# Angle tables spread by TensorE, and the first query projection from rounded parts, in a Trainium2 transformer layer

## The reference

```python
def layer(x):                                  # x is (2, 1024, 512)
    Q = heads(x @ Wq.T + bq)                   # 32 heads of 16
    K = heads(x @ Wk.T + bk)                   # 8 heads of 16
    V = heads(x @ Wv.T + bv)
    Q, K = (t * cos + rot_half(t) * sin for t in (Q, K))
    w = softmax(Q @ repeat(K, 4).T / 4)
    x = layernorm(x + merge(w @ repeat(V, 4)) @ Wo.T + bo)
    h = silu((x @ gate_w.T) * gate_s) * ((x @ up_w.T) * up_s)
    return layernorm(x + (h @ down_w.T) * down_s)
```

## Time and profile before

| | us |
|---|---|
| median of 3 runs | 1018.65 (1018.28 to 1018.89) |
| the profiled execution | 1020.25, with a span of 1018.3 from its first to its last instruction |
| TensorE busy in the span | 1007.7 (99%) |
| VectorE / ScalarE / GpSimd busy | 797.5 / 665.6 / 274.0 |
| first maxima tile on TensorE | 25.51 after the span's start |

### The profile page before, as it was taken

One profiled execution on the slowest core, in us unless ns is written; L12 is line 12 of the kernel. 1 busy time (PEld: TensorE's weight loads), 2 busy tenths in 40 slices (PEclk: granted clock), 3 DMA queues, 4 the chain that ended last, 5 costly groups with the idle time before them and its releaser, 6 DMA issues.

```text
span 1018.3 us, 15671 instructions
## 1 busy us (share of the span) xinstructions
PE 1007.7 (99%) x5852; PEld 533.1 (52%) x5852; DVE 797.5 (78%) x1132; ACT 665.6 (65%) x1345; POOL 274.0 (27%) x284
## 2 busy tenths in 40 slices
PE   9999999999999999999999999999999999999996
PEld 4643435334444333443444433333358888888885
DVE  6999797999787999779899999999713666462635
ACT  5279796888787989779667788888862430222221
POOL 3461030241255541246310063466000001000002
PEclk9999999999999999999999999999999999999999
DMA  6184417234225521444150447331439112221011
GB/s 229 62 214 123 109 55 203 64 93 91 55 84 123 92 85 39 86 112 100 36 81 12 121 140 186 86 104 59 157 107 228 51 42 59 66 66 17 0 42 44
DMA packets 64290, 94.82 MB, mean 93 GB/s; under 512 B 37520, under 2 KB 37776, under 8 KB 62128
## 3 DMA queue, kind: packets, MB, share of 16 engines
q1 hardware_dynamic: 63920, 93.49, 34.9%
q10 hardware_dynamic: 288, 0.26, 0.1%
HBM read 53.88 MB, written 27.00 MB: 79 GB/s over the span
## 4 chain that ended last, share of the span: by engine, by line
PE 96%; DVE 2%; DMA 0%; issue 0%; POOL 0%; DVEq 0%; POOLq 0%
PE PS L478 30%; PE PV L497 25%; PE PSA L567 16%; PE PS L584 6%; PE PSA L456 6%; PE PS L400 4%; PE PS L523 2%; PE PSA L523 2%; PE PV L584 2%; PE PSA L400 2%; DVE nmx L1007 1%; PE PS L437 1%; DMA A<-in_wqk 0%; PE PV L437 0%; PE PS L567 0%; DVE nmx L1003 0%
## 5 line engine op out<-in xcount | busy, mean ns | idle before, releaser
L798 ACT ACTIVATE Bn<-PS 128x512 f32<-128x512 f32 x1128 | 536.2, 558 | 86.5 <-PE PS L478 73.7
L456 PE MATMUL PSA<-Kt,Qt 48*128 48x512 f32 x1010 | 382.9, 459 | 0.5 <-DVE nmx L1007 0.4
L478 PE MATMUL PS<-Qt,Kt 50*128 50x512 f32 x1128 | 381.9, 434 | 0.0
L478 PEld LDWEIGHTS PS<-Qt,Kt 50*128 50x128 f32 x1128 | 183.3, 184 | 302.7 <-ACT Bn L798 277.1
L1003 DVE TENSOR_REDUCE nmx<-PSA 128x1 f32<-128x512 f32 x488 | 310.7, 678 | 29.8 <-PE PSA L456 29.8
L1007 DVE TENSOR_REDUCE nmx<-PSA 128x1 f32<-128x1024 f32 x261 | 317.4, 1218 | 17.9 <-PE PSA L456 15.0
L497 PE MATMUL PV<-Bn 128*32 128x512 f32 x2048 | 272.8, 605 | 0.0
L456 PEld LDWEIGHTS PSA<-Kt,Qt 48*128 48x128 f32 x1010 | 173.0, 183 | 8.7 <-issue 2.2
L567 PE MATMUL PSA<-x1Th,wr 128*128 128x512 f32 x344 | 135.3, 393 | 0.0
L567 PE MATMUL PSA<-x1Tl,wr 128*128 128x512 f32 x344 | 134.3, 390 | 0.0
L834 ACT ACTIVATE sg<-PSA,gs 128x512 f32<-128x512 f32 x43 | 29.7, 690 | 128.1 <-PE PSA L567 128.1
(11 more groups left out here) (174 smaller groups left out, 899.6 us busy)
## 6 DMA issues: line engine op xcount, KB each, us to landing
Qt<-pscr SPq DMA_DIRECT2D x90, 128.0 KB, 5.2
A<-in_wf SPq DMA_DIRECT2D x11, 768.0 KB, 5.8
wr<-A SPq DMA_DIRECT2D x33, 256.0 KB, 2.9
pscr<-A SPq DMA_DIRECT2D x16, 512.0 KB, 3.5
vscr<-Bn SPq DMA_DIRECT2D x32, 256.0 KB, 2.7
Kt<-pscr SPq DMA_DIRECT2D x90, 64.0 KB, 2.8
A<-A SPq DMA_DIRECT2D x16, 256.0 KB, 3.6
Bn<-vscr SPq DMA_DIRECT2D x8, 512.0 KB
```

The costliest lines, as they stand in the source:

```text
L456: op = e.matmul(slot_pair(s)[:, h, :], Qt[n % 3][p:p + NC_, g % 2, 128 * qt:128 * qt + 128], Kt[n % 3][p:p + NC_, 512 * h:512 * h + 512], ...
L478: e.matmul(score_tile(i)[:, cols], Kt[n % 3][rows, 128 * kt:128 * kt + 128], Qt[n % 3][rows, g % 2, 512 * qh + cols.start:512 * qh + cols. ...
L798: e.activation(Pb[c % NP_][:, cols], score_tile(score_bank[c, p])[:, cols], ACT.Exp, scale=0.25).then_inc(*act_exp.next(piece(c, p)))
```

## The change

- **Angles.** `sinT` and `cosT` (1 MB, four loads) are no longer loaded. A table of 24 rows by 2304 bf16 numbers is (110 KB, two loads on ScalarE's queue): eight frequencies, each value as a sum of three bf16 addends, and a 0, 1, -1 pattern. Four bf16 products on TensorE (`spread_angles`, 128 by 512 each) spread and add them into PSUM, and ScalarE copies each to `sinT` or `cosT` (`keep_angles`).
- **Filling products.** A third one of 192 columns is added to the two of 512.
- **Order.** Both halves of K come first (the angle products among them), then both of Q0. The value products of two tiles come in whole ahead of the picks, not in pieces around them.
- **Q0 from parts.** Q0's eight plain products become split ones, 24 records. They need `xh0`/`xl0` of all eight pieces and the parts of `wq0`, which are now made in the opening: `round_w(0)` by ScalarE, `low_x(0)` and `low_x(1)` by VectorE, the other six `low_x` and `low_w(0)` by GpSimd, in a row.
- **Low part of K, half 0** (`low_first(0, 0)`) moves from VectorE to GpSimd, behind that row; `low_w(1)` follows without its wait for VectorE. Four of VectorE's six memsets of `Kt` move to GpSimd.

```diff
-                if b == 0 and m in (0, 4):
+                if b == 0 and m == 4:
                     w.wait_ge(*landed[f"wq{m}"].at())
                     w.wait_ge(*landed[f"xT{h}{k}"].at())
                     pairs = [(wqk[:, m, k, :], xT[:, h, k, :])]
                 elif b == 0:
-                    w.wait_ge(*pool_split.at(("x0", h, k)))
+                    w.wait_ge(*(dve_split if 4 * h + k < 2 else pool_split).at(("x0", h, k)))
                     w.wait_ge(*pool_split.at(("w0", m)))
                     pairs = [(v[m][:, k, :], t[4 * h + k][:, :]) for v, t in ((wh0, xh0), (wl0, xh0), (wh0, xl0))]
...
+            def spread_angles(h):
+                w.wait_ge(*landed[f"angle{h}"].at())
+                for j in range(2):
+                    c = 256 + 1024 * h + 512 * j
+                    e.matmul(bank(2 * h + j), angle[0:24, 128 * j:128 * j + 128], angle[0:24, c:c + 512],
+                             start=True, stop=True).then_inc(*pe_angle.next((h, j)))
...
-            for _ in range(2):
-                e.matmul(PV[:, :], Vflat[:, 0:128], Vflat[:, 0:512], start=True, stop=True)
-            fill(0, 0, 0, 1, 2, 3)
+            for n in (512, 512, 192):
+                e.matmul(PV[:, 0:n], Vflat[:, 0:128], Vflat[:, 0:n], start=True, stop=True)
+            fill(0, 0, 0, 1)
+            spread_angles(0)
+            fill(0, 0, 2, 3)
+            fill(0, 1, 0)
+            spread_angles(1)
+            fill(0, 1, 1, 2, 3)
             fill(1, 0, 0, 1, 2, 3)
-            fill(0, 1, 0, 1, 2, 3)
-            fill(1, 1, 0)
-            pick(0, 0, 0, PSA[:, 0, :], dve_lo.at((0, 0)))
-            fill(1, 1, 1, 2, 3)
-            value_rows(0, 0, 3, (0, 1))
+            fill(1, 1, 0, 1, 2, 3)
+            bank_free[0:4] = [act_angle.at((h, j)) for h in range(2) for j in range(2)]
+            value_rows(0, 0, 3)
+            pick(0, 0, 0, PSA[:, 0, :], pool_lo.at((0, 0)))
+            value_rows(0, 1, 3)
+            pick(0, 1, 0, PSA[:, 1, :], dve_lo.at((0, 1)))
             for a in range(2):
                 pick(1, 0, 2 + 2 * a, bank(2 * a), dve_lo.at((1, 0)))
-            pick(0, 1, 0, PSA[:, 1, :], dve_lo.at((0, 1)))
...
-            value_rows(0, 0, 3, (2, 3))
-            value_rows(0, 1, 3)
...
+            def keep_angles(h):
+                for j, t in enumerate((sinT, cosT)):
+                    w.wait_ge(*pe_angle.at((h, j)))
+                    e.copy(t[:, 512 * h:512 * h + 512], bank(2 * h + j)).then_inc(*act_angle.next((h, j)))
...
-            round_x(0, 1, 2, 3, 4, 5, 6, 7)
+            round_x(0, 1)
+            keep_angles(0)
+            round_x(2)
+            round_w(0)
+            round_x(3, 4, 5)
+            keep_angles(1)
+            round_x(6, 7)
             round_first(0, 0, dve_rope.at((0, 0)))
...
+            round_w(1)
+            round_first(0, 1, dve_rope.at((0, 1)))
+            evacuate_last()
             round_first(1, 0, dve_rope.at((1, 0)))
...
+            low_x(0, 1)
             turn_pairs(0, 0)
+            turn_pairs(0, 1)
             turn_pairs(1, 0)
-            low_first(0, 0)
-            turn_pairs(0, 1)
+            low_first(0, 1)
             low_first(1, 0)
-            low_first(0, 1)
+            place(Kt[0][64:64 + NC_, 512:1024], PSA[64:64 + NC_, 1, :], pe_pick.at((0, 1, 0)), ("k", 1))
             place(Qt[0][:, 1, 0:512], bank(2), pe_pick.at((1, 0, 4)), ("q", 0, 1))
-            place(Kt[0][64:64 + NC_, 512:1024], PSA[64:64 + NC_, 1, :], pe_pick.at((0, 1, 0)), ("k", 1))
...
-            low_x(0, 1, 2, 3)
-            w.wait_ge(*dve_lo.at((0, 1)))
+            for i in (1, 2):
+                for p in (32, 96):
+                    w.wait_ge(*pool_one.at())
+                    e.memset(Kt[i][p:p + 18, :].bitcast(F32), 1.0).then_inc(*pool_one.next())
+            w.wait_ge(*pool_one.at())
+            low_x(2)
+            low_w(0)
+            low_x(3, 4, 5, 6, 7)
+            w.wait_ge(*act_hi.at(("first", 0, 0)))
+            e.tensor_tensor(lo_r[0][:, 0:512], qraw[0][:, 0:512], hi_r[0][:, 0:512].bitcast(F32), ALU.subtract).then_inc(
+                *pool_lo.next((0, 0)))
             low_w(1)
-            low_x(4, 5)
...
             load_rows(0)
             load(wqk[:, 0], wqk_d[:, 0], "wq0")
-            load_angles(0)
             load_rows(1)
             load(sel_in.rearrange("p (m c) -> p m c", m=6), sel_d, "sel")
-            load_angles(1)
```

More of the change, by code:

```diff
@@ L83, in post_ln_layer @@
         wo = sb("wo", [128, KT, 512])
+        base_x1a = 32 * ((nc.sbuf_base + 31) // 32)
         x1a = sb("x1a", [128, 8, 512])
@@ L137, in post_ln_layer @@
               for m, p in enumerate((84608, in_a(2048), in_a(0), in_a(512), 82560))]
+        angle = at("angle", base_x1a - base, [128, 2304], BF16)
         xh0 = [at(f"xh0{j}", 66176 + 2048 * j, [128, 512], F32R) for j in range(8)]
@@ L141, in post_ln_layer @@
         wh0 = {m: at(f"wh0{m}", 82560 + 4096 * (m - 1), [128, KT, 128], F32R) for m in (1, 2, 3)}
+        wh0[0] = at("wh00", 36864, [128, KT, 128], F32R)
         wl0 = {m: at(f"wl0{m}", 84608 + 4096 * (m - 1), [128, KT, 128], F32R) for m in (1, 2, 3)}
+        wl0[0] = at("wl00", 38912, [128, KT, 128], F32R)
         ath = [at(f"ath{k}", in_a(3072 + 1024 * k), [128, 1024], F32R) for k in range(KT)]
@@ L904, in scalar @@
             load(wqk[:, 4], wqk_d[:, 4], "wq4")
+            load(angle[0:24, 0:1280], angle_d[:, 0:1280].bitcast(BF16), "angle0")
             load(bqk[:, :], bqk_d, "bqk")
-            round_x(0, 1, 2, 3, 4, 5, 6, 7)
+            load(angle[0:24, 1280:2304], angle_d[:, 1280:2304].bitcast(BF16), "angle1")
+            round_x(0, 1)
[5 more added lines that the diff above has]
+            round_x(6, 7)
             round_first(0, 0, dve_rope.at((0, 0)))
@@ L960, in turn_pairs @@
                 w.wait_ge(*landed["bqk"].at())
-                w.wait_ge(*landed[f"sin{h}"].at())
-                w.wait_ge(*landed[f"cos{h}"].at())
+                w.wait_ge(*act_angle.at((h, 0)))
+                w.wait_ge(*act_angle.at((h, 1)))
                 for p in (0, 64):
@@ L970, in turn_pairs, with low_x @@
                 e.tensor_tensor(raw, raw, qrot, ALU.subtract).then_inc(*dve_rope.next((i, h)))
+            def low_x(*js):
+                for j in js:
+                    h, k = divmod(j, KT)
+                    w.wait_ge(*act_split.at(("x0", h, k)))
+                    e.tensor_tensor(xl0[j][:, :], xT[:, h, k, :], xh0[j][:, :].bitcast(F32), ALU.subtract).then_inc(
+                        *dve_split.next(("x0", h, k)))
             def low_first(i, h):
@@ L1337, in rope @@
                 w.wait_ge(*swapped_in[j % 2].at(j))
-                for h in range(2):
-                    w.wait_ge(*landed[f"cos{h}"].at())
-                    w.wait_ge(*landed[f"sin{h}"].at())
+                w.wait_ge(*act_angle.at((1, 1)))
                 e.tensor_tensor(raw, raw, cosT, ALU.mult).then_inc(*pool_rope.next((j, "cos")))
@@ L1453, in gpsimd @@
             e.memset(Vflat[:, 512:2208], 1.0).then_inc(*pool_one.next())
-            low_x(0, 1, 2, 3)
-            w.wait_ge(*dve_lo.at((0, 1)))
+            for i in (1, 2):
+                for p in (32, 96):
+                    w.wait_ge(*pool_one.at())
[7 more added lines that the diff above has]
+                *pool_lo.next((0, 0)))
             low_w(1)
-            low_x(4, 5)
             raw, qrot, cos, sin = cols_of(1, 1)
             w.wait_ge(*act_ev.at("swapped"))
-            w.wait_ge(*landed["sin1"].at())
-            w.wait_ge(*landed["cos1"].at())
+            w.wait_ge(*act_angle.at((1, 1)))
             e.tensor_tensor(raw, raw, cos, ALU.mult).then_inc(*pool_cs.next("cos"))
@@ L1468, in gpsimd @@
                 *pool_cs.next("lo"))
-            low_x(6, 7)
             low_w(2)
@@ L1529, in load_rows @@
                     load(xT[:, h, k, :], xT_d[0, h, :, k, :], f"xT{h}{k}")
-            def load_angles(h):
-                c = slice(512 * h, 512 * h + 512)
-                load(sinT[:, c], sin_d[:, c], f"sin{h}")
-                load(cosT[:, c], cos_d[:, c], f"cos{h}")
             def write_parts(b, m, i, hi, lo):
@@ L1712, in sync @@
             load(ident[:, :], id_d, "id")
+            w.wait_ge(*pool_lo.at((0, 0)))
             w.wait_ge(*dve_lo.at((0, 1)))
@@ L1744, in sync @@
                     b, part = x_at[at_u]
+                    w.wait_ge(*pe_angle.at((1, 1)))
                     t = slice(2 * part, 2 * part + 2)
@@ L1806, in select_rows, with bf16_parts @@
     return sel
+def bf16_parts(t):
+    parts = []
+    for _ in range(3):
+        top = (t.view(np.uint32) & np.uint32(0xFFFF0000)).view(np.float32)
+        parts.append(top)
+        t = t - top
+    return parts
 def kernel(**inputs):
@@ L1822 @@
     cos, sin = np.cos(ang).astype(np.float32), np.sin(ang).astype(np.float32)
-    cosT = np.concatenate([np.repeat(cos, 8, 0)] * 2)
-    sinT = np.concatenate([np.repeat(-sin, 8, 0), np.repeat(sin, 8, 0)])
```

(9 more changed lines are left out.)

20 lines of the change are left out of this document (9 added, 11 removed).

## The result

The change made the kernel slower by 2.4 us: 1021.31 us, the median of 20 runs (1020.86 to 1022.39), against 1018.91 for 20 runs of the kernel before (1018.02 to 1021.09). The ratio is 1.0022, with a 95% interval of 1.0016 to 1.0028. That is clear of no difference, but not of the 0.2% (2.0 us) up to which the prediction counts a change as the same. The profiled execution took 1021.24 with a span of 1019.4. The one of before had taken 1020.25 with a span of 1018.3. So the two profiles are 1.0 apart and the medians 2.4.

The account below looks back on a forecast made before the run. TensorE, busy 99% of the span, was taken as the bound, with first maxima as mark. TensorE's 2.0 us saving shrinks to 0.6 through the copy; the port makes it +1.1: 1018.65 + 1.1, say 1019.7, range 1017.2 to 1021.3.

Parts of the forecast that it names:

- the port: Opening: VectorE's five subtractions with both inputs in SBUF and GpSimd's row delay each other; first maxima 26.6 instead of 24.9.
- rival B: Opening: port held, but the third filling product leaves the clock rise at 10.3; first maxima at 27.8, +2.3 us; chance 0.16.
- 3.3 us sooner is 1.6 less: TensorE's opening: third filling product closes the gap, so the higher clock comes at 7.0 instead of 10.3, saving 1.6 us.
- 6.0 the earliest: TensorE's opening: with no gap, the higher clock might come from about 6.0, at the latest at 10.3; 7.0 taken.
- TensorE's own work: Opening: 6.9 us of plain Q0 products removed, 5.6 of split records and 0.9 of angle products added, together -0.4.
- The angle products: TensorE's opening: four products adding 0.9 us, if each is one record like the picks.
- The 24 records at 0.23: TensorE's Q0 fills: split records at the picks' spacing, 5.6 us in place of 6.9 for eight plain products.
- The uncovered copy: After the last pick: VectorE copies `Qt` with no values to cover it, 0.2 to start, 0.69, then 0.28.
- K's second half comes after VectorE is done with the first: VectorE's turning in the opening: K half 0 ends at 13.5, half 1 can start only from 14.4.
- Loads: Opening: dropping sine and cosine loads and adding two angle loads of 110 KB was costed at nothing.

Follow-up runs that it names:

- e4: Changed kernel with VectorE's subtractions reading one input from PSUM and the low part of K half 0 back on VectorE: 1019.63 us, ratio 1.0009.
- e1: Kernel before, unchanged, profiled and measured again: 1019.05 us, ratio 1.0002.
- e2: Kernel before plus only the third filling product of 192 columns: 1018.39 us, ratio 0.9997.
- e3: Changed kernel without its third filling product: 1021.29 us, ratio 1.0028.
- e5: Kernel before in its own order, with angles spread by TensorE instead of loaded, and the third filling product: 1019.91 us, ratio 1.0009.
- e6: Kernel before with GpSimd's low parts moved forward in one row, without the wait for VectorE's last low part: 1020.28 us, ratio 1.0013.
- e7: Changed kernel with Q0 from plain products, GpSimd held behind VectorE's last low part, K half 0's low part on VectorE: 1021.00 us, ratio 1.0016.
- e9: e7 with the second tile's value products moved behind the picks: 1020.52 us, ratio 1.0016.
- e10: e4 with the second tile's value products moved behind the picks: 1019.71 us, ratio 1.0008.

## Why the prediction was right or wrong

The forecast was 1019.7, no change that can be told with a leaning to slower; measured was 1021.31, at the very top of the range, 2.4 above before and so at the edge of the 2.0 us (the interval is 1.6 to 2.9). The main mechanism, the port, was right. That the number still fell inside the range is luck: the range reached so far up for rival B's sake, and B's reason did not hold.

- **The port** was the step on which the sign hung, and it held: L970's successor 1.54 to 1.80 for 0.69 (expected up to 0.69 + 1.24), GpSimd late by 1.0 in its five (2 x 0.55), `xl0[7]` at 19.67 (20.1), a wait of TensorE for it, first maxima at 26.22 (26.6). The forecast's steps were not all met. The second and third L1000 end at 18.52 and 22.71, where 17.6 and 20.7 were stepped out, since the third met `low_w(1)`; the two L1012, forecast as held, ran free, and the last low part ends at 24.09, where 24.3 was forecast. So the waits came earlier in VectorE's row than forecast and added up to the same end. The trace agrees with the Trainium skill's "SBUF — State Buffer", "Who interferes with whom", in both halves of its rule: two inputs in SBUF meet GpSimd (1.54 to 1.80), one in PSUM does not (e4, 0.70). Only three of the five subtractions met GpSimd. The price is 1.1 in the mark, 1.4 at the same clock (1.7 was forecast, from 24.9 to 26.6), and 1.7 in the median (after against e4).
- **The step that failed** is "3.3 us sooner is 1.6 less", credited to the third filling product, and behind it the choice to measure everything against one profile whose clock came up at 10.3. The clock did come up early in the changed kernel, as forecast. But it does so in the kernel before as well, in e1 at about 6.7 without the product, and adding the product to before (e2) or taking it from the changed kernel (e3) moved the medians by -0.14 and -0.02. Nor was 6.0 the earliest: in e2 and e5 the rise is at 4.0 to 4.8. Without that credit the forecast would have been +2.7, and rival B with its +2.3 would have been the likeliest. B had the right size by the wrong cause: it let the changed kernel keep a late rise, where the kernel before has the early one in two of three profiles of this opening (e1, and e6 with the same work on TensorE) and, by its times, mostly: 23 of its 121 runs lie above 1020 us, and the late profile took 1020.25. The Trainium skill's "TensorE: Matmul & The Clock Gate", Part 1, has it that the number of cold products varies from run to run; the prediction cited that and took one trace's rise for before's all the same.
- **TensorE's own work** was put at 0.4 less. Between e1 and e4 the fills end at 19.9 (20.40 less a pick of 0.46) and at 20.21; of this 0.3, 0.2 stands already at the fourth weight load (7.07 and 7.25), so the work is 0.1 more. The angle products are the term: 1.5 for the two pairs, sized at 0.9. The 24 records at 0.23 were right, and Q0 from parts, 1.4 less by the forecast's terms, is worth 1.1 in the mark when the port is not in its way (e7 to e4; medians -1.4, from two rounds).
- **The uncovered copy** was seen and costed (0.2 + 0.69 + 0.28 after the last pick) and measured 0.88 of idle time. That K's second half comes after VectorE is done with the first was in the steps (14.4 against 13.5), but not what it means: in e4, e9 and e10 it is VectorE's last low part that the last picks wait for.
- **Loads** cost nothing, and gave nothing.

In medians, step by step from before: angles and filling product +1.05, K first (with the values ahead of the picks) +1.1, Q0 from parts -1.4, port +1.7, together +2.45. Only the second and the last of these were also measured within one round (e5 and e7; e3 and e4). For the other two the sum leaves open how it is split, by half a microsecond or more. Up to 0.9 us of the differences lies behind the mark, and no experiment was made there.

## What to carry over

Before a forecast is set against one profiled execution, ask whether its own time is near the median: here it was 1.3 us above the median, and the second profile of the same program, with its clock up 3.6 us sooner, was 1.9 us shorter. When work moves from an idle engine to one that shares a port with the critical one, look at where the inputs lie; reading one of them from PSUM took the meeting away, and each subtraction still took 0.70. And moving covered work ahead of a copy takes the copy's cover away.

## Seen of the hardware

- TensorE's clock rose anywhere between 3.2 and 10.6 us after the start in thirteen profiles of an opening that begins at 1.3; in e2, e3 and e5 it did so ahead of the first real product.
- Two bf16 products of 24 rows between float32 ones cost 0.53, and the first float32 record behind them 0.2 more, where two fp32r records in a row cost 0.46.
- VectorE subtracting from PSUM took 0.70 (both inputs in SBUF: 0.69) and wrote to PSUM in 0.76 where it wrote SBUF in 0.75.
